# A two-layer image kernel: last stage with its 192 inner channels divided as 128 and 64, images split in seven strips

## The chip, the core and the metric

The kernel runs on one core of a Trainium2 chip. The metric is the time of the whole program on the device in microseconds (us), the median of the runs. PE is the matrix engine (PEld its weight loads), DVE the vector engine, ACT the scalar engine, POOL the GpSimd engine, SP the engine whose queue issues all the transfers here.

## The reference, cut to what matters

The program applies two layers to 32 images of 56 x 56 pixels with 48 channels: an adapter with a convolution whose weights are generated, then a block with window attention and a feed-forward part. The change lies in the feed-forward part alone:

```python
x = shortcut + o                       # (32, 56, 56, 48), after the attention
y = _layer_norm(x, ln2_g, ln2_b)
y = conv(y, w_ffn1)                    # 3 x 3, 48 -> 192 channels, 'SAME'
y = gelu(y * bn1_scale + bn1_shift)    # exact gelu
y = conv(y, w_ffn2)                    # 1 x 1, 192 -> 48 channels
return x + (y * bn2_scale + bn2_shift)
```

## The kernel before, in words

The program has three stages that follow one another with a barrier between them: the adapter, the attention (which leaves `x2_chunks`, the residual, and `y_chunks`, the normalized input of the feed-forward part, in device memory), and `feed_forward`, the last stage. Only the last is changed.

**Data of an image.** The 48 channels times 3 rows of the 3 x 3 window make 144 values for each pixel. 128 of them stand in the tile `ya` as partitions (three copies of the image, each shifted by a row), the last 16 in `yb`, three times (shifted by a column), so 48 partitions with data, of 64. Each row has 58 columns (`YW`), so an image is 3248 columns. There is one `ya` and one `yb`. Nine transfers fill each of them (`Y_DMAS`).

**Precision.** Matmuls work on a short float format (`F32R`). Each factor is divided into an upper part (a cast, `hi`) and the rest (a subtraction, `lo`), and a product is the sum of hi x hi, lo x hi and hi x lo. The split images `ya_hi`, `ya_lo` and `yb_sp` (hi and lo of `yb` in one tile) exist twice, one for even and one for odd images (`a` is 0 or 1).

**Loops.** An image is worked on in 7 strips of 8 rows, 448 pixels each (`C1` is 7, `T1` is 448). For each strip and each half of the 192 inner channels (k = 0, 1; 96 channels each) `convolve` issues 11 matmuls: three columns of the window times three products from `ya`, and two from `yb_sp`. That is 22 for a strip. ACT computes the gelu of the half (line 1303) and casts it (1306), POOL subtracts (1233), and `feed_back` multiplies hidden values by `wf` in 6 matmuls for the strip (line 1265), one strip behind the convolution. DVE then adds the scaled result to the residual `xr` (line 1365).

**Splitting the next image.** DVE does it in four pieces of a whole image, after the results of strips 1, 2, 3 and 4: cast of `ya` (1330), cast of `yb` (1333), subtraction for `ya` (1336), subtraction for `yb` (1339). When both subtractions are done SP starts to load the image after that into `ya` and `yb`:

```python
sp.wait_ge(y_lo_set, image * 2 + 4)
load_ya(m + 1, a)
load_yb(m + 1, a)
sp.wait_ge(result, image * C1 + C1)
sp.dma_start(out[image, :, :], xr[a][:, :]).then_inc(out_done[a], 16)
```

DVE also adds the constant `t2` to the whole of `xr` once per image (1357). Each engine works through its own instructions in the written order; semaphores join them.

Of the kernel before, what the change touches and what calls it, by code (L numbers as in the profile page):

```python
# [20 lines left out]
F32 = mybir.dt.float32  # L21
# [9 lines left out]
HID = 4 * C  # L31
N = WS * WS
# [30 lines left out]
class Pack:  # L63
# [34 lines left out]
    "wa": (128, 3 * HID), "wb": (PP, HID), "wf2": (HID // 2, 2 * C),  # L98
    "s1": (HID // 2, 2), "t1": (HID // 2, 2), "s2": (C, 1), "t2": (C, 1),
# [1006 lines left out]
def feed_forward(nc, x2s, ys, pack, out):  # L1106
# [7 lines left out]
    with ctx:  # L1114
# [39 lines left out]
        def by_column(tile):  # L1154
            return tile[:, :].rearrange("q (k m) -> q k m", k=3)
# [4 lines left out]
        def _(sp):  # L1160
# [43 lines left out]
            sp.wait_ge(y_lo_set, 2)  # L1204
            load_ya(0, 1)
            load_yb(0, 1)
            with sp.Fori(0, B // 2 - 1) as m:
                for a in range(2):
                    image = m * 2 + a
                    sp.wait_ge(y_lo_set, image * 2 + 4)  # L1210
# [12 lines left out]
        @block.gpsimd  # L1223
        def _(pool):

            for row in (0, H - 1):
                ins = pool.memset(ya[:, row * YW:(row + 1) * YW], 0.0)  # L1227
            ins.then_inc(ya_zeroed, 1)

            def images(m):  # L1230
                for U in range(4 * C1):
                    pool.wait_ge(hid_hi_set, m * (4 * C1) + U + 1)  # L1232
                    pool.tensor_tensor(hid_lo[:, U % slots, :], hid[:, U % slots, :], hid_hi[:, U % slots, :],  # L1233
                                       ALU.subtract).then_inc(hid_lo_set, 1)

            with pool.Fori(0, B // 2) as m:  # L1236
                images(m)

        @block.tensor
        def _(pe):  # L1240
            def convolve(bank, a, c, k):
                rows = slice(c * R1, (c + 1) * R1)
                hidden = slice(k * half, (k + 1) * half)

                def pixels(tile, kw):
                    return tile.rearrange("q (r n) -> q r n", r=H)[:, rows, kw:kw + W]

                for kw in range(3):
                    for i, (weights, image) in enumerate(((wa_hi, ya_hi), (wa_hi, ya_lo), (wa_lo, ya_hi))):
                        pe.matmul(ps_h[bank][0:half, 0:T1], by_column(weights)[:, kw, hidden],  # L1250
                                  pixels(image[a][:, :], kw), start=kw == 0 and i == 0, stop=False)

                pe.matmul(ps_h[bank][0:half, 0:T1], wb_hi[:, hidden], pixels(yb_sp[a][:, :], 0), start=False, stop=False)
                pe.matmul(ps_h[bank][0:half, 0:T1], wb_lo[:, hidden], pixels(yb_sp[a][:, :], 0),  # L1254
                          start=False, stop=True).then_inc(h_mm, 1)

            def feed_back(t, T):

                pe.wait_ge(hid_lo_set, 2 * t + 2)
                if not isinstance(t, int) or t >= 2:  # L1260
                    pe.wait_ge(result, t - 1)
                for k in range(2):
                    slot, m = (2 * T + k) % slots, slice(k * C, (k + 1) * C)
                    for i, (weights, hidden) in enumerate(((wf_hi, hid_hi), (wf_lo, hid_hi), (wf_hi, hid_lo))):
                        mm = pe.matmul(ps_f[T % 2][0:C, 0:T1], weights[:, m], hidden[:, slot, :],  # L1265
                                       start=k == 0 and i == 0, stop=k == 1 and i == 2)
                mm.then_inc(f_mm, 1)

            def images(m):

                for a in range(2):
                    start = isinstance(m, int) and a == 0
                    if start:
                        pe.wait_ge(first_lo_set, 2)
                    else:
                        pe.wait_ge(y_lo_set, m * 4 + a * 2 + 2)
                    for c in range(C1):
                        if start and c == first_rows // R1:
                            pe.wait_ge(y_lo_set, 2)
                        T = a * C1 + c  # L1280
                        t = m * (2 * C1) + T
                        for k in range(2):
                            if not isinstance(m, int) or t * 2 + k >= slots:
                                pe.wait_ge(gelu_done, t * 2 + k - slots + 1)
                            convolve((2 * T + k) % slots, a, c, k)
                        if not isinstance(m, int) or t >= 1:
                            feed_back(t - 1, (T - 1) % (2 * C1))

            pe.wait_ge(w_lo_set, 3)
            images(0)  # L1290
            with pe.Fori(1, B // 2) as m:
                images(m)
            feed_back(B * C1 - 1, 2 * C1 - 1)

        @block.scalar
        def _(act):
            def images(m):
                for U in range(4 * C1):
                    u = m * (4 * C1) + U
                    act.wait_ge(h_mm, u + 1)  # L1300
                    if not isinstance(m, int) or u >= slots:
                        act.wait_ge(f_mm, m * (2 * C1) + (U - slots) // 2 + 1)
                    act.activation(hid[:, U % slots, :], ps_h[U % slots][0:half, 0:T1], ACT.Gelu,  # L1303
                                   bias=w("t1")[:, U % 2:U % 2 + 1], scale=w("s1")[:, U % 2:U % 2 + 1]).then_inc(gelu_done, 1)
                    act.wait_ge(gelu_done, u + 1)
                    act.activation(hid_hi[:, U % slots, :], hid[:, U % slots, :], ACT.Copy).then_inc(hid_hi_set, 1)  # L1306

            act.wait_ge(weights_in, 16)
            images(0)
            with act.Fori(1, B // 2) as m:  # L1310
                images(m)

        @block.vector
        def _(dve):
# [3 lines left out]
            dve.memset(yb[BO // 2:BO, 0:(H - 1) * YW - 2], 0.0).then_inc(yb_zeroed, 1)  # L1318
            dve.wait_ge(weights_in, 16)
            dve.tensor_copy(wa_hi[:, :], w("wa")).then_inc(w_hi_set, 1)  # L1320
            dve.tensor_copy(wb_hi[:, :], w("wb")).then_inc(w_hi_set, 1)
            dve.tensor_copy(wf_hi[:, :], w("wf2")).then_inc(w_hi_set, 1)
            dve.wait_ge(w_hi_set, 3)
            dve.tensor_tensor(wf_lo[:, :], w("wf2"), wf_hi[:, :], ALU.subtract).then_inc(w_lo_set, 1)
            dve.tensor_tensor(wa_lo[:, :], w("wa"), wa_hi[:, :], ALU.subtract).then_inc(w_lo_set, 1)
            dve.tensor_tensor(wb_lo[:, :], w("wb"), wb_hi[:, :], ALU.subtract).then_inc(w_lo_set, 1)


            def split_hi_a(a, px, signal):
                return dve.tensor_copy(ya_hi[a][:, px], ya[:, px]).then_inc(signal, 1)  # L1330

            def split_hi_b(a, px, signal):
                return dve.tensor_copy(yb_sp[a][0:BO, px], yb[:, px]).then_inc(signal, 1)

            def split_lo_a(a, px, signal):
                return dve.tensor_tensor(ya_lo[a][:, px], ya[:, px], ya_hi[a][:, px], ALU.subtract).then_inc(signal, 1)

            def split_lo_b(a, px, signal):
                return dve.tensor_tensor(yb_sp[a][BO:PP, px], yb[0:C, px], yb_sp[a][0:C, px], ALU.subtract).then_inc(signal, 1)  # L1339
# [175 lines left out]
```

## Time and profile before

| | |
|---|---|
| median of three runs | 3990.65 us (3989.6 to 3991.79) |
| profiled execution, its time | 3992.1 us |
| its span | 3990.3 us |
| last stage in that span | from 2627.4 us to the end |
| mean granted clock of PE, share of full speed | 0.972 |
| busy, share of the span | PE 93%, DVE 61%, ACT 59%, POOL 56% |

The busy shares are means over three stages. Matmuls overlap in the pipeline: each lasts about 0.37 us in the records, while the next one starts about 0.2 us after it, so what counts is the distance between starts. Times in the rows are from the start of the span.

### The profile page before, as it was taken

Reading aid. Unit: us, or ns where it says so; the run is one execution under the profiler, and the core shown is the slowest. Engines: PE = TensorE matmul, PEld = TensorE weight load, DVE = VectorE, ACT = ScalarE, POOL = GpSimd, SP = SyncE. Lnnn points to the kernel's source line nnn. Section 1 sums busy time; section 2 is a strip of 40 time slices with the busy share of each in tenths; the row PEclk is TensorE's granted clock in tenths of the full one; section 3 lists DMA queues with packets and bytes.
Section 4 is the critical chain, followed back from the end, with each engine's and each line's share of the span. In section 5 each row is a group of like instructions: output and inputs, shape, how many; then the busy total and the mean of one; then the engine's idle time right before and its main releaser. Section 6 shows DMA issues by size and latency. Waiting matters only on the chain. (4 is left out here: it accounts for less than half of the span.)

```text
span 3990.3 us, 95518 instructions
## 1 busy us (share of the span) xinstructions
PE 3711.8 (93%) x33140; PEld 2678.4 (67%) x33140; DVE 2432.0 (61%) x3923; ACT 2334.6 (59%) x4212; POOL 2240.8 (56%) x2186
## 2 busy tenths in 40 slices
PE   6889789999999999999999999959999999999999
PEld 3556566666666666666666666647777777777776
DVE  4544367777777777777777777743444434444343
ACT  3343167777777777777777777734444444444444
POOL 1111156666666666666666666635655656556564
PEclk7898899999999999999999999979999999999999
DMA  4331111111111111111111111145445454454542
GB/s 105 97 97 48 56 32 37 37 37 37 37 37 39 38 38 38 37 37 37 37 37 37 39 38 38 35 72 99 76 86 88 70 98 75 86 88 70 98 75 47
DMA packets 235743, 229.73 MB, mean 58 GB/s; under 512 B 118064, under 2 KB 230704, under 8 KB 232624
## 3 DMA queue, kind: packets, MB, share of 16 engines
q1 hardware_dynamic: 235696, 229.14, 28.2%
q8 instruction: 26, 0.43, 0.0%
q14 instruction: 21, 0.17, 0.0%
HBM read 151.26 MB, written 77.76 MB: 57 GB/s over the span
## 5 line engine op out<-in xcount | busy, mean ns | idle before, releaser
L1233 POOL TENSOR_TENSOR hid_lo<-hid,hid_hi 96x448 fp32r<-96x448 f32 x448 | 771.2, 1727 | 583.5 <-ACT hid_hi L1306 583.5
L613 POOL TENSOR_TENSOR kex<-ks,cw 112x294 f32<-112x294 f32 x1024 | 734.3, 752 | 232.1 <-ACT ks L865 232.1
L1303 ACT ACTIVATE hid<-ps_h,cw 96x448 f32<-96x448 f32 x448 | 324.0, 723 | 728.0 <-PE ps_h L1254 728.0
L1365 DVE SCALAR_TENSOR_TENSOR xr<-ps_f,cw,xr 48x448 f32<-48x448 f32 x224 | 151.3, 676 | 773.2 <-PE ps_f L1265 773.2
L673 PE MATMUL ps_s<-kex,qbd 112*98 112x294 f32 x2048 | 591.9, 410 | 0.0
L1250 PE MATMUL ps_h<-ya_hi,wa_hi 128*96 128x448 f32 x1344 | 501.4, 373 | 30.1 <-DVE yb_sp L1339 30.1
L1250 PE MATMUL ps_h<-ya_hi,wa_lo 128*96 128x448 f32 x1344 | 498.4, 371 | 0.0
L1250 PE MATMUL ps_h<-ya_lo,wa_hi 128*96 128x448 f32 x1344 | 498.2, 371 | 0.0
L1012 DVE TENSOR_TENSOR s<-ps_s,bias 98x294 f32<-98x294 f32 x1024 | 434.9, 454 | 14.1 <-PE ps_s L673 2.1
L673 PEld LDWEIGHTS ps_s<-kex,qbd 112*98 112x98 f32 x2048 | 318.0, 165 | 165.8 <-issue 80.2
L888 ACT ACTIVATE pt<-ps_t 98x588 f32<-98x588 f32 x512 | 338.6, 661 | 120.1 <-PE ps_t L684 114.5
L1024 DVE TENSOR_REDUCE mx<-s 98x12 f32<-98x588 f32 x512 | 390.7, 763 | 13.2
L1028 DVE TENSOR_TENSOR s<-s,mx 98x588 f32<-98x588 f32 x384 | 388.6, 1012 | 13.1
L684 PEld LDWEIGHTS ps_t<-cw,s 98*98 98x98 f32 x3072 | 300.3, 126 | 101.7 <-issue 46.5
L881 ACT ACTIVATE s<-s 98x588 f32<-98x588 f32 x512 | 354.4, 692 | 4.2 <-DVE s L1028 1.1
L684 PE MATMUL ps_t<-cw,s 98*98 98x98 f32 x3072 | 347.8, 248 | 1.3 <-ACT lnv L901 1.3
L699 PEld LDWEIGHTS ps_o<-vs,pt 98*49 98x49 f32 x12288 | 303.2, 126 | 66.1 <-issue 53.4
L699 PE MATMUL ps_o<-vs,pt 98*49 98x18 f32 x12288 | 328.5, 199 | 0.0
L1250 PEld LDWEIGHTS ps_h<-ya_hi,wa_hi 128*96 128x96 f32 x1344 | 216.8, 161 | 102.4 <-issue 30.7
L744 PEld LDWEIGHTS ps_m<-wvs,h 112*98 112x98 f32 x2048 | 197.9, 167 | 108.7 <-issue 100.9
L1306 ACT ACTIVATE hid_hi<-hid 96x448 fp32r<-96x448 f32 x448 | 259.1, 578 | 14.3
L1250 PEld LDWEIGHTS ps_h<-ya_hi,wa_lo 128*96 128x96 f32 x1344 | 217.2, 162 | 65.3
(152 smaller groups left out, 6767.4 us busy)
## 6 DMA issues: line engine op xcount, KB each, us to landing
ya<-y_chunks SPq DMA_DIRECT2D x64, 532.9 KB, 6.4
y_chunks<-y SPq DMA_DIRECT2D x256, 76.1 KB, 1.8
xin<-x_chunks SPq DMA_DIRECT2D x256, 73.5 KB, 2.5
xres<-x_chunks SPq DMA_DIRECT2D x256, 73.5 KB, 1.9
x_chunks<-xo SPq DMA_DIRECT2D x256, 73.5 KB, 1.8
out<-xr SPq DMA_DIRECT2D x32, 588.0 KB, 8.2
yb<-y_chunks SPq DMA_DIRECT2D x96, 177.6 KB, 8.2
xr<-x_chunks SPq DMA_DIRECT2D x32, 514.5 KB, 5.6
```

The source lines that it names most:

```text
L613: pool.tensor_tensor(kex[a][:, win, :, :], ks[:, win, :].unsqueeze(1).to_broadcast([PP, HEADS, N]), w("head").unsqueeze(2).to_broadcast([P ...
L673: pe.matmul(ps_s[win % 3][0:2 * N, 0:HN], qbd[a][:, win, :], kex[a][:, win, :, :].rearrange("c h k -> c (h k)"), start=True, stop=True).th ...
L684: mm = pe.transpose(ps_t[0:2 * N, i, part], s_sb[d % 2][:, i, part], w("ident"))
L699: mm = pe.matmul(ps_o[BO * img:BO * img + N, (i * (HEADS // 2) + j) * VW:(i * (HEADS // 2) + j + 1) * VW], pt[win // 2][:, win % 2, j, img ...
L881: act.activation(s_sb[d % 2][:, :, :], s_sb[d % 2][:, :, :], ACT.Exp).then_inc(exp_done, 1)
L888: act.activation(pt[d][:, :, :, :, :].rearrange("q w j i n -> q w (j i n)"), ps_t[0:2 * N, :, 0:HN], ACT.Copy).then_inc(pt_set, 1)
L1012: dve.tensor_tensor(s_sb[i][:, k, :], ps_s[win % 3][0:2 * N, 0:HN], bias[:, low, int(win == NWC - 1), :], ALU.add).then_inc(s_biased, 1)
L1024: dve.tensor_reduce(mxi, s4, AX.X, ALU.max).then_inc(max_done, 1)
L1028: dve.tensor_tensor(s4, s4, mxi.unsqueeze(2).to_broadcast([2 * N, 2 * HEADS, N]), ALU.subtract).then_inc(shifted, 1)
L1233: pool.tensor_tensor(hid_lo[:, U % slots, :], hid[:, U % slots, :], hid_hi[:, U % slots, :], ALU.subtract).then_inc(hid_lo_set, 1)
L1250: pe.matmul(ps_h[bank][0:half, 0:T1], by_column(weights)[:, kw, hidden], pixels(image[a][:, :], kw), start=kw == 0 and i == 0, stop=False)
L1303: act.activation(hid[:, U % slots, :], ps_h[U % slots][0:half, 0:T1], ACT.Gelu, bias=w("t1")[:, U % 2:U % 2 + 1], scale=w("s1")[:, U % 2:U ...
```

## The change: what it does

- The inner channels are divided as 128 (part a) and 64 (part b) instead of 96 and 96. For part b the upper and lower halves of the weights stand side by side in one tile (`wa_both`, `wb_both`, 2 x 64 columns). One matmul with `ya_hi` then gives hi x hi in 64 rows of the result and lo x hi in the other 64. Part b takes 7 matmuls (`convolve_b`), part a 11 (`convolve_a`).
- ACT copies the other 64 rows of part b out of the matmul's result (`upper_half`), DVE adds the two halves (`add_halves_b`), and the gelu reads the sum.
- `feed_back` has the halves of `wf` side by side too: 3 matmuls, two strips behind the convolution, and its result stands in two halves that DVE adds one after the other (`add_result`, two instructions).
- The image is split in seven strips of 464 columns, one in each slot (a slot is the work for one strip of results), instead of four whole-image pieces. Casts and the subtraction for `yb` stay on DVE, the subtraction for `ya` goes to POOL (`split_lo_a`). POOL keeps the subtraction for part a of the hidden values; that for part b is on DVE.
- The constant `t2` is added by ACT, strip by strip (`add_shift`).
- SP loads the next `ya` when all seven strips are subtracted (`y_a_set`), and `yb` on `y_b_set`. There is still one `ya` and one `yb`.

```diff
+            sp.wait_ge(y_a_set, image * slices + 2 * slices)
             load_ya(m + 1, a)
+            sp.wait_ge(y_b_set, image * slices + 2 * slices)
             load_yb(m + 1, a)
...
         @block.gpsimd
...
+            def split_lo_a(image, a, s):
+                pool.wait_ge(ya_hi_set, image * slices + s + 1)
+                pool.tensor_tensor(ya_lo[a][:, strip(s)], ya[:, strip(s)], ya_hi[a][:, strip(s)], ALU.subtract).then_inc(y_a_set, 1)
...
+            def slots(m, last):
+                for T in range(images):
...
+                    if started(t, 1):
+                        hidden_lo(t - 1, (T - 1) % images)
...
+                    if not (last and a == 1):
+                        split_lo_a(m * 2 + a + 1, 1 - a, c)
...
         @block.tensor
...
+            def convolve_b(t, T, a, c):
+                if started(t, 2):
+                    pe.wait_ge(b_added, t - 1)
+                bank = ps_b[T % 2]
+                pe.matmul(bank[:, 0:T1], wb_both[:, :], pixels(yb_sp[a][:, :], c, 0), start=True, stop=False)
+                for kw in range(3):
+                    pe.matmul(bank[0:HB, 0:T1], wa_both[:, kw, 0:HB], pixels(ya_lo[a][:, :], c, kw), start=False, stop=False)
+                for kw in range(3):
+                    mm = pe.matmul(bank[:, 0:T1], wa_both[:, kw, :], pixels(ya_hi[a][:, :], c, kw), start=False, stop=kw == 2)
+                mm.then_inc(b_mm, 1)
...
+                    elif c == 0:
+                        pe.wait_ge(y_a_set, (m * 2 + a) * slices + slices)
+                        pe.wait_ge(y_b_set, (m * 2 + a) * slices + slices)
+                    convolve_b(t, T, a, c)
+                    convolve_a(t, T, a, c)
+                    if started(t, 2):
+                        feed_back(t - 2, (T - 2) % images)
...
         @block.scalar
...
+            def slots(m):
+                for T in range(images):
+                    t = m * images + T
+                    upper_half(t, T)
+                    if started(t, 1):
+                        hidden_a(t - 1, (T - 1) % images)
+                        add_shift(m if T >= 1 else m - 1, (T - 1) % images)
+                    hidden_b(t, T)
...
         @block.vector
...
+            def split(image, a, s):
+                px = strip(s)
+                if s == 0:
                     dve.wait_ge(ya_in, image * (Y_DMAS * 16) + Y_DMAS * 16)
+                dve.tensor_copy(ya_hi[a][:, px], ya[:, px]).then_inc(ya_hi_set, 1)
+                if s == 0:
                     dve.wait_ge(yb_in, image * (Y_DMAS * 16) + Y_DMAS * 16)
+                dve.tensor_copy(yb_sp[a][0:BO, px], yb[:, px]).then_inc(yb_hi_set, 1)
+                dve.wait_ge(yb_hi_set, image * slices + s + 1)
+                dve.tensor_tensor(yb_sp[a][BO:PP, px], yb[0:C, px], yb_sp[a][0:C, px], ALU.subtract).then_inc(y_b_set, 1)
...
+            def slots(m, last):
+                for T in range(images):
+                    t = m * images + T
+                    if started(t, 3):
+                        add_result(t - 3, (T - 3) % images)
+                    if started(t, 1):
+                        hidden_lo(t - 1, (T - 1) % images)
+                    a, c = T // C1, T % C1
+                    add_halves_b(t, T)
+                    if not (last and a == 1):
+                        split(m * 2 + a + 1, 1 - a, c)
```

On DVE, in the loop over images, this stood around the start of a split before (`ya_in` and `yb_in` count landed transfers, `f_mm` finished `feed_back`s):

```order
L1357 TENSOR_SCALAR xr<-xr,cw 48x3136 [waits x2_in0]
L1361 ISA
L1363 ISA [waits shift_added]
L1365 SCALAR_TENSOR_TENSOR xr<-ps_f,cw,xr 48x448 [waits f_mm]
L1363 REGISTER_ALU
L1365 SCALAR_TENSOR_TENSOR xr<-ps_f,cw,xr 48x448 [waits f_mm]
L1343 ISA
L1330 CAST ya_hi<-ya 128x3248 [waits ya_in]
L1363 REGISTER_ALU
L1365 SCALAR_TENSOR_TENSOR xr<-ps_f,cw,xr 48x448 [waits f_mm]
L1333 CAST yb_sp<-yb 64x3248 [waits yb_in]
```

And this stands there now, from the first strip of an image's slots (where the split of the next image starts) into the second:

```order
L1423 SCALAR_TENSOR_TENSOR xr<-ps_f,cw,xr 48x448 [waits f_mm,shift_added]
L1426 SCALAR_TENSOR_TENSOR xr<-ps_f,cw,xr 48x448 [waits f_half_added]
L1415 TENSOR_TENSOR hid_b_sp<-hid_b,hid_b_sp 64x448 [waits b_hi_set]
L1410 REGISTER_ALU
L1411 TENSOR_TENSOR pre<-ps_b,small 64x448 [waits small_set]
L1401 ISA
L1402 CAST ya_hi<-ya 128x464 [waits ya_in]
L1405 CAST yb_sp<-yb 64x464 [waits yb_in]
L1406 ISA
L1407 TENSOR_TENSOR yb_sp<-yb,yb_sp 48x464 [waits yb_hi_set]
L1423 SCALAR_TENSOR_TENSOR xr<-ps_f,cw,xr 48x448 [waits f_mm,shift_added]
```

The wait for the transfers moved from the second strip of an image to its first, and results and sums of later strips stand behind it.

POOL, in its loop, had one kind of work before:

```order
L1233 TENSOR_TENSOR hid_lo<-hid,hid_hi 96x448 [waits hid_hi_set]
L1232 REGISTER_ALU
L1233 TENSOR_TENSOR hid_lo<-hid,hid_hi 96x448 [waits hid_hi_set]
L1232 REGISTER_ALU
L1233 TENSOR_TENSOR hid_lo<-hid,hid_hi 96x448 [waits hid_hi_set]
```

and has two kinds in turn now:

```order
L1248 TENSOR_TENSOR hid_a_lo<-hid_a,hid_a_hi 128x448 [waits a_hi_set]
L1243 ISA
L1244 TENSOR_TENSOR ya_lo<-ya,ya_hi 128x464 [waits ya_hi_set]
L1247 REGISTER_ALU
L1248 TENSOR_TENSOR hid_a_lo<-hid_a,hid_a_hi 128x448 [waits a_hi_set]
```

The number of its instructions for a strip stays at two; the second one of a slot now follows DVE's cast of the same strip, and releases the loads.

## Rows read from the trace of the kernel before

**Rows 1.** The page: span, and each engine's busy time (share, instructions).
```profile
span 3990.3 us, 95518 instructions
PE 3711.8 (93%) x33140; PEld 2678.4 (67%) x33140; DVE 2432.0 (61%) x3923; ACT 2334.6 (59%) x4212; POOL 2240.8 (56%) x2186
```
**Rows 2.** Busy time by stretch: one image, twenty images; clock, DMA share, GB/s last.
```profile
3024.60:3066.10 41.50, 40.90 (x197) 29.90 (x196) 17.55 (x12) 18.22 (x28) 24.28 (x15) 1.00 0.47 83
3066.10:3901.00 834.90, 822.84 (x3939) 600.78 (x3937) 351.67 (x241) 365.70 (x562) 489.11 (x282) 1.00 0.48 83
```
**Rows 3.** Timeline of PE (start, duration, line): first matmuls of two strips.
```profile
3001.70 0.37 PE L1250 MATMUL ps_h<-ya_hi,wa_hi 128*96 128x448 f32 x1
...
3007.51 0.38 PE L1250 MATMUL ps_h<-ya_hi,wa_hi 128*96 128x448 f32 x1
```
**Rows 4.** Groups by line, 2700 to 3900 us: count | busy, mean ns | idle before.
```profile
L1303 ACT ACTIVATE hid<-ps_h,cw 96x448 f32<-96x448 f32 x404 | 292.2, 723 | 661.0 <-PE ps_h L1254 661.0
L1306 ACT ACTIVATE hid_hi<-hid 96x448 fp32r<-96x448 f32 x404 | 233.6, 578 | 12.9
```
**Rows 5.** Timeline of SP's queue: first ya, last ya, last yb transfer; next image's first.
```profile
3024.61 0.33 SPq L1170 DMA_DIRECT2D ya<-y_chunks  x1
3028.51 0.32 SPq L1179 DMA_DIRECT2D ya<-y_chunks  x1
3032.89 0.32 SPq L1179 DMA_DIRECT2D yb<-y_chunks  x1
3066.15 0.33 SPq L1170 DMA_DIRECT2D ya<-y_chunks  x1
```
**Rows 6.** Tile yb: time from a transfer's issue to its landing.
```profile
DMA to landing us min/median/max: 6.7/8.1/10.8
```
**Rows 7.** Timeline of DVE at the stage's start: split of the first rows.
```profile
2643.01 0.64 DVE L1330 CAST ya_hi<-ya 128x928 fp32r<-128x928 f32 x1 [7.29 <-DMA ya<-y_chunks]
2643.69 1.13 DVE L1336 TENSOR_TENSOR ya_lo<-ya,ya_hi 128x928 fp32r<-128x928 f32 x1
2648.82 0.64 DVE L1333 CAST yb_sp<-yb 64x928 fp32r<-64x928 f32 x1 [4.00 <-DMA yb<-y_chunks]
```
**Rows 8.** Timeline of DVE in the loop.
```profile
3001.90 0.68 DVE L1365 SCALAR_TENSOR_TENSOR xr<-ps_f,cw,xr 48x448 f32<-48x448 f32 x1 [5.15 <-PE ps_f L1265]
3002.50 1.83 DVE L1330 CAST ya_hi<-ya 128x3248 fp32r<-128x3248 f32 x1
3014.14 3.52 DVE L1336 TENSOR_TENSOR ya_lo<-ya,ya_hi 128x3248 fp32r<-128x3248 f32 x1
3020.89 3.54 DVE L1339 TENSOR_TENSOR yb_sp<-yb,yb_sp 48x3248 fp32r<-48x3248 f32 x1
```
**Rows 9.** The page's groups: a DVE sum with one input from PSUM.
```profile
L1012 DVE TENSOR_TENSOR s<-ps_s,bias 98x294 f32<-98x294 f32 x1024 | 434.9, 454 | 14.1 <-PE ps_s L673 2.1
```
**Rows 10.** Timeline of POOL beside rows 8.
```profile
3002.09 3.27 POOL L1233 TENSOR_TENSOR hid_lo<-hid,hid_hi 96x448 fp32r<-96x448 f32 x1 [1.08 <-ACT hid_hi L1306]
3005.67 1.15 POOL L1233 TENSOR_TENSOR hid_lo<-hid,hid_hi 96x448 fp32r<-96x448 f32 x1 [0.32 <-ACT hid_hi L1306]
3013.74 7.16 POOL L1233 TENSOR_TENSOR hid_lo<-hid,hid_hi 96x448 fp32r<-96x448 f32 x3 [1.08 <-ACT hid_hi L1306]
```
**Rows 11.** Timelines of POOL and DVE in the attention stage, then that DVE line's min/median/max ns.
```profile
2549.69 1.02 POOL L621 TENSOR_TENSOR y<-xc,rstd 112x392 f32<-112x392 f32 x1 [1.68 <-ACT rstd L907]
2550.02 1.32 DVE L1028 TENSOR_TENSOR s<-s,mx 98x588 f32<-98x588 f32 x1
L1028 DVE TENSOR_TENSOR s<-s,mx x384: 770/773/1341, 519.4 to 2600.5; 98x588 f32<-98x588 f32 x192
```
**Rows 12.** Stretches at the start of the stage's matmuls; columns as in rows 2.
```profile
2650.80:2654.20 3.40, 3.40 (x10) 2.55 (x10) 3.40 (x3) 0.00 (x0) 0.00 (x0) 0.50 0.42 63
2654.20:2658.00 3.80, 3.80 (x20) 2.94 (x19) 3.77 (x2) 3.08 (x4) 0.41 (x1) 1.00 0.02 4
```
**Rows 13.** Timelines of DVE and SP: last result, last transfer.
```profile
3984.07 0.68 DVE L1365 SCALAR_TENSOR_TENSOR xr<-ps_f,cw,xr 48x448 f32<-48x448 f32 x1 [2.15 <-PE ps_f L1265]
3984.77 0.34 SPq L1219 DMA_DIRECT2D out<-xr  x1
```

More of the change, by code:

```diff
@@ L31 @@
 HID = 4 * C
+HA, HB = 128, HID - 128
 N = WS * WS
@@ L1239, in _, with pixels @@
+            pool.wait_ge(weights_in, 16)
+            for s in range(slices):
+                split_lo_a(0, 0, s)
+            slots(0, False)
+            with pool.Fori(1, B // 2 - 1) as m:
+                slots(m, False)
+            slots(B // 2 - 1, True)
+            hidden_lo(LAST, images - 1)
         @block.tensor
         def _(pe):
[L1241 to L1246, printed above, removed]
+            def pixels(tile, c, kw):
+                return tile.rearrange("q (r n) -> q r n", r=H)[:, c * R1:(c + 1) * R1, kw:kw + W]
@@ L1248, in convolve, with convolve_a @@
+            def convolve_a(t, T, a, c):
+                if started(t, 2):
+                    pe.wait_ge(gelu_a_done, t - 1)
+                bank = ps_a[T % 2]
                 for kw in range(3):
                     for i, (weights, image) in enumerate(((wa_hi, ya_hi), (wa_hi, ya_lo), (wa_lo, ya_hi))):
-                        pe.matmul(ps_h[bank][0:half, 0:T1], by_column(weights)[:, kw, hidden],
-                                  pixels(image[a][:, :], kw), start=kw == 0 and i == 0, stop=False)
@@ L1253, in convolve @@
-                pe.matmul(ps_h[bank][0:half, 0:T1], wb_hi[:, hidden], pixels(yb_sp[a][:, :], 0), start=False, stop=False)
-                pe.matmul(ps_h[bank][0:half, 0:T1], wb_lo[:, hidden], pixels(yb_sp[a][:, :], 0),
-                          start=False, stop=True).then_inc(h_mm, 1)
+                        pe.matmul(bank[:, 0:T1], weights[:, kw, :], pixels(image[a][:, :], c, kw), start=kw == 0 and i == 0, stop=False)
+                pe.matmul(bank[:, 0:T1], wb_hi[:, :], pixels(yb_sp[a][:, :], c, 0), start=False, stop=False)
@@ L1257, in feed_back @@
+                pe.matmul(bank[:, 0:T1], wb_lo[:, :], pixels(yb_sp[a][:, :], c, 0), start=False, stop=True).then_inc(a_mm, 1)
             def feed_back(t, T):
-                pe.wait_ge(hid_lo_set, 2 * t + 2)
-                if not isinstance(t, int) or t >= 2:
+                pe.wait_ge(b_lo_set, t + 1)
+                pe.wait_ge(a_lo_set, t + 1)
+                if started(t, 2):
                     pe.wait_ge(result, t - 1)
[L1262 to L1287, printed above, removed]
@@ L1291, in _, with hidden_a @@
+            pe.wait_ge(w_lo_set, 6)
+            slots(0)
             with pe.Fori(1, B // 2) as m:
-                images(m)
-            feed_back(B * C1 - 1, 2 * C1 - 1)
+                slots(m)
+            feed_back(LAST - 1, images - 2)
+            feed_back(LAST, images - 1)
         @block.scalar
         def _(act):
[L1297 to L1306, printed above, removed]
+            def hidden_a(t, T):
+                act.wait_ge(a_mm, t + 1)
+                if started(t, 2):
+                    act.wait_ge(a_lo_set, t - 1)
+                act.activation(hid_a[:, T % 2, :], ps_a[T % 2][:, 0:T1], ACT.Gelu, bias=w("t1a"), scale=w("s1a")).then_inc(gelu_a_done, 1)
+                act.wait_ge(gelu_a_done, t + 1)
+                if started(t, 2):
+                    act.wait_ge(f_mm, t - 1)
+                act.activation(hid_a_hi[:, T % 2, :], hid_a[:, T % 2, :], ACT.Copy).then_inc(a_hi_set, 1)
@@ L1308, in _ @@
             act.wait_ge(weights_in, 16)
-            images(0)
+            slots(0)
             with act.Fori(1, B // 2) as m:
-                images(m)
+                slots(m)
+            hidden_a(LAST, images - 1)
+            add_shift(B // 2 - 1, images - 1)
         @block.vector
@@ L1324, in _ @@
[L1324 to L1333, printed above, removed]
@@ L1359, in image_done @@
-            def image_done(m, a, split_next):
-                image = m * 2 + a
-                dve.wait_ge(shift_added, image + 1)
-                for c in range(C1):
-                    dve.wait_ge(f_mm, image * C1 + c + 1)
-                    cols = slice(c * T1, (c + 1) * T1)
-                    dve.scalar_tensor_tensor(out=xr[a][:, cols], in0=ps_f[(a * C1 + c) % 2][0:C, 0:T1], scalar=w("s2"),
-                                             in1=xr[a][:, cols], op0=ALU.mult, op1=ALU.add).then_inc(result, 1)
-                    if split_next and 1 <= c <= 4:
-                        split(image + 1, 1 - a, c - 1)
@@ L1391, in program @@
+            for s in range(slices):
+                split(0, 0, s)
+            slots(0, False)
+            with dve.Fori(1, B // 2 - 1) as m:
+                slots(m, False)
+            slots(B // 2 - 1, True)
+            add_result(LAST - 2, images - 3)
+            hidden_lo(LAST, images - 1)
+            add_result(LAST - 1, images - 2)
+            add_result(LAST, images - 1)
 def program(nc, x, pack1, pack2, pack3, out):
```

164 lines of the change are left out of this document (93 added, 71 removed).

## The prediction, written before the changed kernel ran

> **What bounds the kernel now.** I read the page first: PE is busy 93% of the span [rows 1]. Then the last stage by stretches: in one image of it, and in twenty, PE is busy for 98.5% at a full clock, while DVE, ACT and POOL stand at 42 to 59% [rows 2]. PE is the bound there. The timeline gives its price: 5.81 us between the first matmuls of two strips, with 28 matmuls between (22 and 6), so 0.2075 us for each [rows 3]. An image takes 41.54 us, from one first `ya` transfer to the next [rows 5], though 7 x 5.81 is 40.7: PE waits about 0.9 us for POOL. Last I read the transfers, since the change moves their wait.
>
> **What PE gains.** A strip has 7 + 11 + 3 = 21 matmuls now: 21 x 0.2075 = 4.36 us, 30.5 us an image. Weight loads of 128 columns are not in the trace of this stage; those of 96 hide behind the matmuls, and I leave the distance at 0.2075. If this were still the bound, each image would save 11 us. I don't think it will be.
>
> **DVE's strip.** The casts: 0.64 us for 928 columns, 1.83 for 3248 [rows 7, 8], so 0.40 for 464. The subtraction: 1.13 and 3.52, so 0.65 for 464 and 0.63 for 448 [rows 7, 8]. The sum with one input from PSUM: 0.454 for 294 columns [rows 9], at the same slope 0.61 for 448. A result costs 0.68 [rows 8], now twice. Together 0.68 + 0.68 + 0.63 + 0.61 + 0.40 + 0.40 + 0.65 = 4.05. An instruction with nothing to wait for starts 0.08 before the end of the last (3001.90 + 0.68 against 3002.50); that applies to 5 of the 7. One that waits for its predecessor starts 0.04 later [rows 7]; that applies to 2. So 4.05 - 0.40 + 0.08 = 3.73 us a strip, under PE's 4.36.
>
> **ACT's strip.** Gelu 0.72 twice, casts 0.58 twice [rows 4], two more instructions of about 0.58: 3.8 us with the waits inside it. It has cover, and it hides the copy and the shift. `add_shift` moves off DVE for nothing.
>
> **The wait that takes over.** There is one `ya` and one `yb`. Before, DVE split an image after results 1 to 4, and about three strips passed between the last subtraction (3020.89 + 3.54 = 3024.43) and the next cast that needs the loaded data, which hid the load. Now the seventh strip is split in the seventh slot and the first strip of the next image in the very next slot, so the whole load stands open. Its length: 0.2 us until SP issues (3024.43 to 3024.61), 8.28 us from the first `ya` transfer to the last `yb` transfer [rows 5], 8.1 us until that lands [rows 6]: 16.6 us. Behind the waiting cast on DVE stand the cast and subtraction of `yb`, then results, `hidden_lo` and sums of the next strips. PE can go on for about two and a half strips, until `feed_back` wants the `hidden_lo` that stands behind the wait. PE cannot start the next image either, since it wants all seven strips of it split.
>
> So an image is now one loop: load, then what is left of the first strip (cast 0.40 and subtraction 0.65 of `yb`, 1.0 with the overlaps), then six slots of DVE, whose last cast frees POOL's last subtraction, which releases the load. With six slots at 3.73 and the last subtraction of POOL ending 0.3 after the slot, that is 16.6 + 1.0 + 22.4 + 0.3 = 40.3 us, hardly under the 41.54 of before. PE's work fits in it with 10 us to spare.
>
> **POOL and DVE get in each other's way.** A subtraction on POOL takes 1.15 us alone. One that met a cast of 1.83 us on DVE took 3.27, and three that met a subtraction of 3.52 us took 7.16, where 3 x 1.15 is 3.45 [rows 8, 10]: POOL stands still while DVE casts or subtracts. It goes the other way too: line 1028 takes 0.77 us at its best, and 1.32 in the place where a POOL instruction had begun 0.33 us before; it was held until about 2550.57, just before that one ended at 2550.71 [rows 11]. So these two cannot run together, while a result or the sum (one input from PSUM) can run beside POOL. A slot has 0.63 + 0.40 + 0.40 + 0.65 = 2.08 us of exclusive DVE work and two POOL subtractions of about 1.07 us hold each (the 3.27 ended 1.03 after the cast). Who goes first decides the slot:
> - If the subtraction for `ya`, ready when the first cast ends, gets its turn in the gap between the cast of `yb` and the subtraction of `yb` (DVE waits there for its own cast), DVE loses 1.05 us in each slot. POOL's other subtraction meets `hidden_lo` or the cast every second slot: another 0.1 or 0.4. Slots of about 4.85 and 5.25, 5.0 in the mean and 4.8 for the first, whose hidden work is already done: 29.8 for six.
> - If it waits for the end of the slot, it runs beside the two results, and only the other one costs DVE 0.5: five slots of 4.25 and one of 3.73, 25.0.
>
> I take the first, because the instruction that waits longest is POOL's, and line 1028 was held for nearly the whole of what was left of a POOL instruction. The Trainium skill, page "SBUF — State Buffer", section "Who interferes with whom", says that whoever issues first keeps the shared ports for the whole instruction and the other blocks fully. Rows 11 agree. Rows 10 agree less: POOL's instruction is recorded 0.41 us before DVE's cast and yet stood still. By the rule the time is the 4162 us below, by a right of way for DVE the 4061.
>
> **The sum.** Loop of an image: 16.6 + 1.0 + 29.8, less 0.4 since POOL's last subtraction ends before DVE's: 47.0 us. Start: the first cast of `yb` could begin at 2648.82 [rows 7]; 1.0 for the first strip, then six strips back to back at 0.32 + 0.32 + 1.07 + 0.57 = 2.3, all exclusive: released at about 2663. Thirty-one loops: 1457. The last image has no split, so PE sets it: 30.5, and 2 for a halved clock after the wait (the first 3.4 us of the stage's matmuls ran at 0.50, then it rose to 1.00 [rows 12]; PE's gap of some 6 us will let it fall again, elsewhere hidden by the spare). Then the tail of the last strip: 10 us (gelu, cast and POOL's subtraction 2.5, `feed_back` 0.8, two results 1.4, transfer out 5.5, from 3984.77 to the span's end at 3990.3 [rows 1, 13]). Span: 2663 + 1457 + 42.5 = 4162.5. The profiled execution lasted 1.8 us more than its span, and its 3992.1 stands 1.45 above the median; so 4163 as a median.
>
> **Rivals.**
> - B, DVE keeps its turn: 16.6 + 1.0 + 25.0 + 1.1 = 43.7 an image; 2663 + 31 x 43.7 + 42.5 + 0.4 = 4061. For it: rows 10. Against it: rows 11.
> - C, the other side: POOL's work falls into DVE's waits and costs nothing, so the loop is the 40.3 above, start at 2658. 2658 + 1249 + 42.5 = 3950, faster. It decides below 41.5 an image, that is if contention costs less than 0.2 us a slot, or if the load lands some 3 us sooner. Against it: 2.08 + 2.14 us of exclusive work in a slot of 3.73.
> - D, PE stays the bound because the load hides after all: 30.5 to 31 an image, 3670. The order of the waits speaks against it.
> - E, the clock stays at half for most of an image: 7 x 8.7 = 61 an image, about 4600. For it: PE idle for a third of the loop. Against it: the rise after 3.4 us of work in rows 12.
> - F, dearer meetings (each DVE instruction held, 5.7 a slot): 51 an image, 4290.
>
> **Chances and range.** My forecast 45%, B 25%, C 14%, D 3%, E 4%, F 9%. Unknown costs: slot 3.73 to 5.7, load 15 to 17.5 us (31 us for each us). The range goes from the middle of C to short of F, 3955 to 4260; for slower cases alone 4020 to 4230. A change below 0.2% (8 us) could not be told from none. Faster: most of C, and D, 15%; within: 3%; slower: 82%.
>
> **What would show it.** In the new profile DVE waits some 12 us for the `yb` transfers once an image, the first `ya` transfers stand about 47 us apart (43.7 for B, 40.3 for C), PE's busy share in the stage falls to two thirds, and the subtraction of `yb` for a strip starts about 1.1 us after the cast before it. No wait for the transfers would prove the central step wrong. A distance of matmuls above 0.3 us would make PE a bound again.

## The result, and the profile after

The changed kernel takes 4264.3 us (median of 4 runs, 4261.3 to 4266.9) against 3990.6 us (4 runs, 3989.6 to 3991.8): 1.0685 times as long, 95% interval 1.0667 to 1.0704. The forecast was slower, 4163 us, with 3955 to 4260 as the range: the direction and the cause held, the size was 101 us short, and the time lies 4 us above the range.

The page of the changed kernel, its span and engines, answers to [rows 1]:

```profile
span 4264.7 us, 93986 instructions
PE 3550.4 (83%) x31572; PEld 2623.3 (62%) x31572; DVE 3028.0 (71%) x5111; ACT 2583.7 (61%) x4660; POOL 2008.3 (47%) x2186
```

PE lost 161 us of work and the span grew by 274, so no engine's busy time tells why. The stretches do (columns as in [rows 2]; twenty-nine images of the last stage, then three stretches of 4 us around the start of one):

```profile
2707.10:4168.80 1461.70, 1045.43 (x4263) 816.84 (x4263) 1053.45 (x1422) 756.60 (x1218) 488.41 (x406) 0.86 0.42 69
3076.00:3080.00 4.00, 0.06 (x1) 0.06 (x1) 3.09 (x6) 0.00 (x0) 0.00 (x0) 0.74 0.00 0
3080.00:3084.00 4.00, 4.00 (x11) 3.09 (x12) 3.90 (x6) 3.31 (x6) 1.34 (x2) 0.50 0.00 0
3084.00:3088.00 4.00, 4.00 (x19) 3.33 (x18) 3.90 (x6) 2.12 (x4) 2.37 (x2) 0.91 0.72 141
```

PE is busy for 71.5% of the stage where it was 98.5%. After 4.7 us without work (from 3075.2 to 3079.9) its granted clock is at 0.50, the lower level, for 4 us, and 0.91 in the next four. DVE, too, is busy for only 72%: no engine is the bound, a loop through several is. SP's queue (start, duration; the loop's first transfer, then first `ya` and last `yb` of one image, the first of the next, and the last image's) answers to [rows 5]:

```profile
2660.44 0.32 SPq L1180 DMA_DIRECT2D ya<-y_chunks  x1
...
3060.35 0.33 SPq L1180 DMA_DIRECT2D ya<-y_chunks  x1
...
3068.70 0.32 SPq L1189 DMA_DIRECT2D yb<-y_chunks  x1
...
3110.80 0.33 SPq L1180 DMA_DIRECT2D ya<-y_chunks  x1
...
4168.75 0.33 SPq L1180 DMA_DIRECT2D ya<-y_chunks  x1
```

From the first to the last of these, 30 images, the first transfers stand 50.3 us apart in the mean (forecast 47.0, before 41.5). DVE's timeline over the same image, from the load's end into the slots:

```profile
3072.50 0.40 DVE L1402 CAST ya_hi<-ya 128x464 fp32r<-128x464 f32 x1 [7.38 <-DMA ya<-y_chunks]
3076.75 0.39 DVE L1405 CAST yb_sp<-yb 64x464 fp32r<-64x464 f32 x1 [3.84 <-DMA yb<-y_chunks]
...
3077.84 0.68 DVE L1423 SCALAR_TENSOR_TENSOR xr<-ps_f,cw,xr 48x448 f32<-48x448 f32 x1
...
3082.74 0.68 DVE L1423 SCALAR_TENSOR_TENSOR xr<-ps_f,cw,xr 48x448 f32<-48x448 f32 x1
...
3084.17 1.40 DVE L1415 TENSOR_TENSOR hid_b_sp<-hid_b,hid_b_sp 64x448 fp32r<-64x448 f32 x1
3085.60 0.62 DVE L1411 TENSOR_TENSOR pre<-ps_b,small 64x448 f32<-64x448 f32 x1
3086.14 0.38 DVE L1402 CAST ya_hi<-ya 128x464 fp32r<-128x464 f32 x1
3086.45 0.39 DVE L1405 CAST yb_sp<-yb 64x464 fp32r<-64x464 f32 x1
3086.87 1.52 DVE L1407 TENSOR_TENSOR yb_sp<-yb,yb_sp 48x464 fp32r<-48x464 f32 x1
3088.42 0.68 DVE L1423 SCALAR_TENSOR_TENSOR xr<-ps_f,cw,xr 48x448 f32<-48x448 f32 x1
```

The load takes 16.4 us from the first transfer to the cast of `yb`, and DVE stands idle for 11.2 of them. Then come the rest of the first strip (1.1 us), a first slot of 4.90, and five of 5.68 (3082.74 to 3088.42), where 5.0 was expected. The subtraction of `yb` takes 1.52 us instead of 0.64, and `hidden_lo` (line 1415) takes 1.40 where it takes 0.62 alone. What POOL did in that slot:

```profile
3083.94 1.14 POOL L1248 TENSOR_TENSOR hid_a_lo<-hid_a,hid_a_hi 128x448 fp32r<-128x448 f32 x1 [1.73 <-ACT hid_a_hi L1338]
3086.60 1.29 POOL L1244 TENSOR_TENSOR ya_lo<-ya,ya_hi 128x464 fp32r<-128x464 f32 x1 [1.52 <-DVE ya_hi L1402]
```

POOL's instruction is recorded first in both meetings (by 0.23 and 0.27 us) and ends 0.5 us before DVE's, which needs 0.62 or 0.64 alone. The views by line (min/median/max in ns) say that this is the rule and no accident of one slot:

```profile
L1407 DVE TENSOR_TENSOR yb_sp<-yb,yb_sp x224: 634/1510/1530, 2646.7 to 4217.7; 48x464 fp32r<-48x464 f32 x112
...
L1415 DVE TENSOR_TENSOR hid_b_sp<-hid_b,hid_b_sp x224: 609/1405/1442, 2677.5 to 4254.4; 64x448 fp32r<-64x448 f32 x112
```

The waits from 2800 to 4000 us (in total, times, longest), 24 images long:

```profile
PE ps_b L1277 <- DVE yb_sp L1407: 186.5, 24, 7.8
DVE ya_hi L1402 <- DMA ya<-y_chunks: 175.4, 24, 7.7
DVE yb_sp L1405 <- DMA yb<-y_chunks: 91.6, 24, 4.4
PE ps_f L1301 <- DVE hid_b_sp L1415: 97.7, 24, 5.0
```

Once an image DVE waits for the load, PE for the last of seven strips, and PE again for the `hidden_lo` that stands behind DVE's wait.

### The profile page after: what moved, and what is told of

It is laid out like the page before. It is cut to its first block and busy times, and to the rows that moved or that the text cites. A ratio compares the mean times of both kernels' runs of the same rounds, so it can differ in the third digit from the quotient of the medians.

```text
span 4264.7 us, 93986 instructions
## 1 busy us (share of the span) xinstructions
PE 3550.4 (83%) x31572; PEld 2623.3 (62%) x31572; DVE 3028.0 (71%) x5111; ACT 2583.7 (61%) x4660; POOL 2008.3 (47%) x2186
## 5 line engine op out<-in xcount | busy, mean ns | idle before, releaser
L1244 POOL TENSOR_TENSOR ya_lo<-ya,ya_hi 128x464 fp32r<-128x464 f32 x224 | 283.3, 1265 | 622.2 <-DVE ya_hi L1402 622.2
L1346 ACT ACTIVATE hid_b<-pre,cw 64x448 f32<-64x448 f32 x224 | 170.2, 760 | 573.9 <-DVE pre L1411 573.9
L1248 POOL TENSOR_TENSOR hid_a_lo<-hid_a,hid_a_hi 128x448 fp32r<-128x448 f32 x224 | 257.1, 1148 | 469.5 <-ACT hid_a_hi L1338 469.5
L1290 PE MATMUL ps_a<-ya_hi,wa_hi 128*128 128x448 f32 x672 | 278.4, 414 | 73.2 <-ACT hid_a L1334 73.0
L1277 PE MATMUL ps_b<-yb_sp,wb_both 112*128 112x448 f32 x224 | 104.5, 466 | 274.9 <-DVE yb_sp L1407 270.1
L1407 DVE TENSOR_TENSOR yb_sp<-yb,yb_sp 48x464 fp32r<-48x464 f32 x224 | 310.2, 1385 | 7.8
L1290 PE MATMUL ps_a<-ya_lo,wa_hi 128*128 128x448 f32 x672 | 265.0, 394 | 0.0
L1415 DVE TENSOR_TENSOR hid_b_sp<-hid_b,hid_b_sp 64x448 fp32r<-64x448 f32 x224 | 259.9, 1160 | 7.0
L1290 PE MATMUL ps_a<-ya_hi,wa_lo 128*128 128x448 f32 x672 | 261.0, 388 | 0.0
```

Source lines behind the costliest of these rows:

```text
L1244: pool.tensor_tensor(ya_lo[a][:, strip(s)], ya[:, strip(s)], ya_hi[a][:, strip(s)], ALU.subtract).then_inc(y_a_set, 1)
L1248: pool.tensor_tensor(hid_a_lo[:, T % 2, :], hid_a[:, T % 2, :], hid_a_hi[:, T % 2, :], ALU.subtract).then_inc(a_lo_set, 1)
L1290: pe.matmul(bank[:, 0:T1], weights[:, kw, :], pixels(image[a][:, :], c, kw), start=kw == 0 and i == 0, stop=False)
```

## The experiments

All are changes of one or two things in the changed kernel ("the base" below, 4264 us, 50.3 us an image). Two doubts led them: is the open load the cause of the loss, and what are the 5.68 us of a slot made of?

**Two tiles each for ya and yb.** Loads run a whole image ahead.

```diff
-        ya = sb("ya", [128, H * YW])
-        yb = sb("yb", [BO, H * YW])
+        ya = [sb(f"ya{a}", [128, H * YW]) for a in range(2)]
+        yb = [sb(f"yb{a}", [BO, H * YW]) for a in range(2)]
...
             sp.wait_ge(y_a_set, slices)
-            load_ya(0, 1)
+            load_ya(1, 0)
```

> The changed kernel with two tiles each for ya and yb, so that an image is loaded a whole image ahead; order and number of DVE's and POOL's instructions unchanged. Theory (the loop of an image is load + first strip + six slots, and the 16.5 us load stands open): the load goes, seven slots of 5.69 us are left, 39.8 us an image, 2660 + 31 x 39.8 + 46 = 3940 us, faster than before the change. Rival (PE at half clock and its own waits set the time, the load only fills time that is lost anyway): 47 us an image or more, above 4150.

Measured: 3921 us (3918 to 3925, 4 runs), 0.983 of before (0.982 to 0.985). One more buffer gives back 343 us: the open load is what made the change a loss. What is left, by the waits from 2800 to 3800 us and by DVE's timeline (lines have moved: 1418 is the subtraction of `yb`, 1426 `hidden_lo`, 1416 the cast of `yb`):

```profile
PE ps_b L1286 <- DVE yb_sp L1418: 164.7, 26, 6.4
```

```profile
3064.84 0.62 DVE L1426 TENSOR_TENSOR hid_b_sp<-hid_b,hid_b_sp 64x448 fp32r<-64x448 f32 x1
...
3066.34 1.35 DVE L1416 CAST yb_sp<-yb 64x464 fp32r<-64x464 f32 x1
3067.72 1.52 DVE L1418 TENSOR_TENSOR yb_sp<-yb,yb_sp 48x464 fp32r<-48x464 f32 x1
```

Now DVE sets the pace, busy for 89% of the stage: most slots take 5.1 to 5.9 us, one of an image 4.4, and one 6.4 or 7.3, in which DVE waits for what PE starts late. That makes 39.2 us an image; the time is 19 us under what I expected. A meeting that misses `hidden_lo` holds the cast instead.

**The casts in another order.** `yb` is cast and subtracted first, `ya` cast last, so POOL's subtraction for `ya` becomes ready when DVE turns to results, which read PSUM.

```diff
-                dve.tensor_copy(ya_hi[a][:, px], ya[:, px]).then_inc(ya_hi_set, 1)
...
                 dve.tensor_tensor(yb_sp[a][BO:PP, px], yb[0:C, px], yb_sp[a][0:C, px], ALU.subtract).then_inc(y_b_set, 1)
+                if s == 0:
+                    dve.wait_ge(ya_in, image * (Y_DMAS * 16) + Y_DMAS * 16)
+                dve.tensor_copy(ya_hi[a][:, px], ya[:, px]).then_inc(ya_hi_set, 1)
```

> The changed kernel with DVE's order in a strip turned: cast of yb, subtraction of yb, then cast of ya, so that POOL's subtraction for ya becomes ready after DVE's last exclusive instruction. Theory (POOL takes its turn in DVE's gap and holds the subtraction of yb for 0.87 us a slot): that hold goes, slots of 4.6 to 4.8, 46 us an image, about 4130. Rival (the subtraction lasts 1.5 us for another reason, its shape or partitions): 4264 as before and 1.5 us still.

Measured: 4128.6 us, 1.035 of before (1.033 to 1.037). From the third on, a slot is 4.33 us (DVE):

```profile
3059.94 0.62 DVE L1415 TENSOR_TENSOR hid_b_sp<-hid_b,hid_b_sp 64x448 fp32r<-64x448 f32 x1
3060.59 0.62 DVE L1411 TENSOR_TENSOR pre<-ps_b,small 64x448 f32<-64x448 f32 x1
3061.13 0.70 DVE L1402 CAST yb_sp<-yb 64x464 fp32r<-64x464 f32 x1
3061.86 0.64 DVE L1404 TENSOR_TENSOR yb_sp<-yb,yb_sp 48x464 fp32r<-48x464 f32 x1
3062.53 0.40 DVE L1407 CAST ya_hi<-ya 128x464 fp32r<-128x464 f32 x1
3062.85 0.67 DVE L1423 SCALAR_TENSOR_TENSOR xr<-ps_f,cw,xr 48x448 f32<-48x448 f32 x1
```

and POOL in it:

```profile
3060.30 1.28 POOL L1248 TENSOR_TENSOR hid_a_lo<-hid_a,hid_a_hi 128x448 fp32r<-128x448 f32 x1 [0.41 <-ACT hid_a_hi L1338]
3063.01 1.21 POOL L1244 TENSOR_TENSOR ya_lo<-ya,ya_hi 128x464 fp32r<-128x464 f32 x1 [1.44 <-DVE ya_hi L1407]
```

The subtraction of `yb` is back at 0.64 us. POOL's work for `ya` runs beside the results, whose 0.67 and 0.69 us are unchanged. Its hidden subtraction runs beside the sum (0.62, unchanged) and holds only the cast, by 0.31; `hidden_lo`, which is recorded 0.36 us before it, keeps its 0.62. So two-SBUF-input instructions and casts are held, and those with an input from PSUM are not. Six slots take 26.7 us in place of 33.3 (the first two are 4.86 and 4.52 long, since POOL is late from the first strip and holds `hidden_lo` and then the cast for longer). That saves 6.6 us, and an image only 4.4: POOL's last subtraction now ends 1.3 us after the slot instead of 0.5 before it (1.8 back), and the cast of `ya` stands behind the load too (0.3). So the 4130 that I had expected is in part luck: the slots are shorter than the 4.6 to 4.8 of that sum, 4.45 in the mean, and what comes back at the end of an image was not in it.

**POOL's subtraction for the hidden values cut short**, first alone, then with the one for `ya`. These kernels leave out lo parts of the products, so they serve to measure and not to use.

```diff
-                pool.tensor_tensor(hid_a_lo[:, T % 2, :], hid_a[:, T % 2, :], hid_a_hi[:, T % 2, :], ALU.subtract).then_inc(a_lo_set, 1)
+                pool.tensor_tensor(hid_a_lo[:, T % 2, 0:8], hid_a[:, T % 2, 0:8], hid_a_hi[:, T % 2, 0:8], ALU.subtract).then_inc(a_lo_set, 1)
...
```

> The changed kernel with only POOL's subtraction of the hidden values cut to 8 columns (that lo part is left out). Theory (each of POOL's two instructions holds one of DVE's): the subtraction of the hidden values on DVE returns from 1.41 to 0.62 us, that of yb stays at 1.5, slots of 4.9 us, 46.3 us an image, about 4140. Rival (POOL's backlog is the cause, so that one shorter instruction frees both): slots near 4.0 us, below 4050.

Measured: 4139.9 us, 1.038 of before (1.036 to 1.040). DVE:

```profile
3059.82 0.68 DVE L1424 SCALAR_TENSOR_TENSOR xr<-ps_f,cw,xr 48x448 f32<-48x448 f32 x1
...
3061.25 0.62 DVE L1416 TENSOR_TENSOR hid_b_sp<-hid_b,hid_b_sp 64x448 fp32r<-64x448 f32 x1
...
3063.17 1.53 DVE L1408 TENSOR_TENSOR yb_sp<-yb,yb_sp 48x464 fp32r<-48x464 f32 x1
3064.73 0.68 DVE L1424 SCALAR_TENSOR_TENSOR xr<-ps_f,cw,xr 48x448 f32<-48x448 f32 x1
```

`hidden_lo` takes 0.62 us, the slot 4.91. That meeting cost 0.78 in five slots of 31 images, 121 us, and 124 are gone. The other one stays at 1.53. Both cut short:

> The changed kernel with both of POOL's subtractions cut to 8 columns (the lo parts of ya and of the 128 hidden channels are left out, their tiles are zero). Theory (POOL holds DVE for 0.87 + 0.80 us a slot, and the load stands open whatever the slots cost): slots of 4.0 us, 16.5 + 1.1 + 24.2 = 42 us an image, 4000 to 4010, still not faster than before the change. Rival (holds do not matter because PE or ACT paces the slot): 47 us or more, above 4150.

Measured: 3968.0 us, 0.995 of before (0.993 to 0.997). I had expected at least 4000, not faster than before. The slots are as expected, but POOL's short last subtraction ends 0.65 us before the next result (at 3059.30, the result at 3059.95), so the load is released sooner: an image takes 41.0 us for 42. DVE's timeline, and its longest wait from 2800 to 3800 us:

```profile
3039.86 0.68 DVE L1429 SCALAR_TENSOR_TENSOR xr<-ps_f,cw,xr 48x448 f32<-48x448 f32 x1
...
3043.21 0.64 DVE L1413 TENSOR_TENSOR yb_sp<-yb,yb_sp 48x464 fp32r<-48x464 f32 x1
3043.88 0.68 DVE L1429 SCALAR_TENSOR_TENSOR xr<-ps_f,cw,xr 48x448 f32<-48x448 f32 x1
```

```profile
DVE ya_hi L1408 <- DMA ya<-y_chunks: 204.0, 24, 8.9
```

The slot without any meeting is 4.02 us, not the 3.73 that I had built from durations. Meetings cost 296 us together, 172 of them the one with the subtraction of `yb` (6 x 31 x 0.88 = 164); the load is as open as before. Without meetings and with the open load the kernel is half a per cent faster than before; without the open load but with meetings, 1.7.

**The split later.** One buffer, no strip split in the first three slots, then 1, 2, 2, 2, so that the load has slots to hide behind.

```diff
+        strips_in_slot = [[], [], [], [0], [1, 2], [3, 4], [5, 6]]
...
-                        split(m * 2 + a + 1, 1 - a, c)
+                        for s in strips_in_slot[c]:
+                            split(m * 2 + a + 1, 1 - a, s)
```

> The changed kernel with one buffer, but the seven strips split in the last four slots of an image (1, 2, 2 and 2) and none in the first three. Theory: the load then runs beside three slots and more of other work, some 14 of its 16.5 us are covered, 39 to 41 us an image, 3930 to 3990. If instead the work on DVE and POOL sets the time wherever the split stands (a sum of 5.69 x 7 = 39.8 plus crowding), the same 39.8 is its floor too; if the load is not the cause, 50 us an image and 4260.

Measured: 4024.0 us, 1.009 of before (1.007 to 1.011), 42.5 us an image: 34 us over the upper end of what I expected. DVE waits for no transfer any more, so that step is right. The slots with two strips are dearer than I had put them (DVE; 1404 is the cast of `ya`, 1409 the subtraction of `yb`), and PE waits for their end (waits from 2800 to 3800 us):

```profile
3020.13 1.47 DVE L1409 TENSOR_TENSOR yb_sp<-yb,yb_sp 48x464 fp32r<-48x464 f32 x1
3021.64 1.29 DVE L1404 CAST ya_hi<-ya 128x464 fp32r<-128x464 f32 x1
...
3023.27 1.52 DVE L1409 TENSOR_TENSOR yb_sp<-yb,yb_sp 48x464 fp32r<-48x464 f32 x1
```

```profile
PE ps_b L1279 <- DVE yb_sp L1409: 222.1, 23, 9.7
```

Three meetings in a slot of 8.25 us (first results at 3016.57 and 3024.82): POOL's hidden subtraction, begun at 3019.95, holds the first, and its two for `ya`, begun at 3021.07 and 3023.01, the others. An earlier slot shows a meeting the other way round, which I come back to below.

**Two buffers and the new order together**, the edits of the first two experiments.

> Both edits together: two tiles each for ya and yb, and in a strip the cast and subtraction of yb ahead of the cast of ya. Theory (load and holds are the two costs and add up): DVE's slot of 4.3 us is below PE's 4.4, so PE is the bound again, with a wait of about 1 us at the start of each image for the last strip's subtraction on POOL: 32 us an image, 2655 + 31 x 32 + 45 = 3690. Rival (the two edits save the same time): about 3790 to 3920.

Measured: 3779.5 us (3777 to 3788, 4 runs), 0.948 of before (0.946 to 0.950). The direction is right, the size 90 us off. The savings of the two edits add up, as the theory had it: 343 and 136 make 479, and 485 are measured. What is off is the wait at the start of an image. PE's timeline at the start of an image shows what I had left out:

```profile
3007.30 0.74 PE L1286 MATMUL ps_b<-yb_sp,wb_both 112*128 112x448 f32 x1 [2.99 <-POOL ya_lo L1253]
```

PE waits for the seventh strip, the last thing that POOL does in an image, though it needs the first. That pause costs more than itself: in the 2.8 us behind it (3007.30 to 3010.10) PE's granted clock is 0.50 and it starts 8 matmuls, for which it needs 1.7 us at the upper level. I had put the pause at 1 us and the clock at nothing.

**PE waits for one strip at a time**, on top of that.

```diff
...
-                    elif c == 0:
-                        pe.wait_ge(y_a_set, (m * 2 + a) * slices + slices)
-                        pe.wait_ge(y_b_set, (m * 2 + a) * slices + slices)
+                    pe.wait_ge(y_a_set, (m * 2 + a) * slices + c + 1)
+                    pe.wait_ge(y_b_set, (m * 2 + a) * slices + c + 1)
```

> As both edits together, and PE waits for the one strip that it is about to read instead of all seven at the start of an image. Theory: the wait at the start of an image goes, 21 matmuls at 0.208 us set the time: 30.8 us an image, 2655 + 31 x 30.8 + 45 = 3655. Rival (PE is paced by ACT or DVE in every slot, not at the start of an image): no difference from both edits together.

Measured: 3659.8 us (3654 to 3663, 4 runs), 0.917 of before (0.916 to 0.919). A stretch of 700 us in its last stage (columns as in [rows 2]):

```profile
2800.00:3500.00 700.00, 700.00 (x3342) 589.65 (x3341) 673.92 (x1115) 596.08 (x955) 372.60 (x319) 1.00 0.65 111
```
PE is busy throughout at the upper clock, an image takes 30.8 us (forecast for a bound PE: 30.5), a slot 4.38 (casts of `yb` at 3011.40 and 3015.78), and DVE has 4% left. This is the version to keep: it beats both kernels.

**The same waits without one of the other two edits.** First one buffer with the new order and the waits strip by strip:

> One ya and one yb, casts of yb first, and PE waits for one strip instead of seven at the start of an image. My theory: while the load is open, the loop of an image is load and DVE's slots, and PE is not on it; so when PE may start changes nothing: 45.7 us an image and 4128 us, as with the order alone, within 5 us. Rival: PE's late start also delays what DVE does behind the load (DVE waited 2.9 us an image for the sum with one buffer), then 43 us an image and about 4045.

Measured: 4121.6 us, 1.033 of before (1.030 to 1.036): 7 us less than with the order alone, where I had allowed 5; the rival's 4045 is far off. While the load is open, it hardly matters when PE may start. Then two buffers, the waits strip by strip, and the casts in the base's order:

> Two tiles each for ya and yb, PE waits for one strip instead of seven, the casts of ya first as in the changed kernel. My theory: DVE's slot with both meetings, 5.7 us, is the bound once nothing else is: 7 x 5.7 = 39.9 us an image less the slots that miss a meeting, so about 39 us and 3920, hardly another time than two buffers alone. Rival: the wait for seven strips was what the 39.2 us hung on, then 7 x 4.9 = 34.3 and about 3770.

Measured: 3934.3 us, 0.986 of before (0.983 to 0.989), 14 more than I said. Its stretch:

```profile
2800.00:3500.00 700.00, 579.60 (x2581) 426.90 (x2580) 679.67 (x862) 460.66 (x738) 298.83 (x247) 1.00 0.53 86
```

DVE's slot is the base's, 5.68 us (first results at 3065.47 and 3071.15). Seven of them make 39.8; the first transfers stand 39.9 us apart. DVE is the bound, at 97%. So the order of three instructions is worth 274 us here (3934 to 3660) and 136 where the load is open.

## Why the forecast had the direction and not the size

- **PE no longer the bound, its distance unchanged.** Right: matmuls stand 0.21 us apart at a full clock. The halved clock after each pause costs nothing in the loop, as said, since PE idles 28% of it (DVE's one wait behind PE, 1.75 us for `small` at 3062.8, ends before the load has landed); E falls with the 0.91 in the second four microseconds.
- **The load stands open.** Right, and within 0.2 us: 16.4 measured and 16.6 in the sum, which held a reaction of 0.2. Two buffers took it away and with it 343 us. Of the rivals, D falls by this.
- **POOL wins the gap before the subtraction of yb.** Right, and it cost a little less: 0.88 us in place of 1.05. B, in which DVE keeps its turn, falls. The sign that I had named is not there as written: the subtraction is recorded 0.03 us after the end of the cast, and the hold stands in its length, 1.52 us. The rule of the Trainium skill that the forecast leaned on (page "SBUF — State Buffer", section "Who interferes with whom": the first to issue keeps the shared ports, the other blocks) agrees with these slots, where POOL is recorded first each time. It agrees the other way round too. In the run with the late split DVE's subtraction is recorded 0.04 us ahead; it keeps its 0.64 us, and POOL's lasts 1.61 in place of 1.15:

```profile
3015.53 0.64 DVE L1409 TENSOR_TENSOR yb_sp<-yb,yb_sp 48x464 fp32r<-48x464 f32 x1
3015.57 1.61 POOL L1249 TENSOR_TENSOR hid_a_lo<-hid_a,hid_a_hi 128x448 fp32r<-128x448 f32 x1 [3.27 <-ACT hid_a_hi L1340]
```

  In these meetings the order of two starts decides, be it by hundredths of a microsecond, and not a right of way of either engine; those of [rows 10] stay the exception.
- **Six slots at 29.8 us: the step that failed.** They take 33.3 (4.90 and five of 5.68), and 31 times the 3.3 us by which the loop is longer are the 101 us; the start (2660.4 for 2663) and the tail (45.6 for 42.5) cancel. Per slot of 5.68 in place of 5.0:
  - The meeting with `hidden_lo`: 0.78 in each of them, where I had 0.1 or 0.4, 0.22 in my mean (5.0 - 3.73 - 1.05): +0.56. (The 4.85 and 5.25 of the forecast have 5.05 as their mean, not 5.0, which is 8 us of the time.) I had let it drift from slot to slot and fall mostly on the cast. It doesn't drift. ACT begins the gelu when DVE's sum is done (3080.54 in the slot above) and frees POOL 3.3 us later; DVE reaches `hidden_lo` 3.6 us after the same sum. Both chains start from one event, so POOL is 0.2 to 0.3 us ahead each time:

```profile
3080.57 0.76 ACT L1346 ACTIVATE hid_b<-pre,cw 64x448 f32<-64x448 f32 x1 [9.54 <-DVE pre L1411]
...
3083.29 0.58 ACT L1338 ACTIVATE hid_a_hi<-hid_a 128x448 fp32r<-128x448 f32 x1
```

  - The bare slot: 4.02 and not 3.73, +0.29. I gave five of seven instructions an overlap of 0.08 us. Only two have it (3085.60 + 0.62 against 3086.14, and the cast behind it); the others start 0.02 to 0.03 after the end. Those three write at another partition than the instruction before: in the base a result behind the subtraction that writes at partition 64 starts 0.03 late (3086.87 + 1.52, then 3088.42; the same with no meeting, 3043.21 + 0.64, then 3043.88), while in the other order, behind the cast that writes at partition 0, the same result starts 0.08 early (3062.53 + 0.40, then 3062.85). The Trainium skill, page "VectorE: DVE Perf Modes", section "Two Vector instructions with no wait between them", gives a model in which a held instruction starts only when every earlier one has finished, and in which one is held, among other conditions, when its output starts in another quadrant (32 partitions) than the last output. The rows fit it; no run moved an output to test it. For the sum the input from PSUM starts at another partition than the last one too (0 after 64), which is another of the page's conditions, so only the result and `hidden_lo` speak for the output alone.
  - The meeting with the subtraction of `yb`: 0.88 for 1.05, -0.17.
- **Rival C, without meetings faster than before at 3950.** Its slot was too kind. The 0.29 us that the bare slot lacked are 54 us in six slots of 31 images, more than the 41 that C gained, so C comes to an estimated 4004. With both meetings gone the time was 3968, half a per cent faster, because the short instructions also save elsewhere: POOL's last subtraction ends 0.65 us before the next result and not 0.3 after it, 29 us in all, and the first release of the load comes at 2651.5 for 2658.
- **Rival F, 5.7 us a slot, 4290.** This is what happened, for its price: 5.68. I had given it 9% and let the range end short of it. Its mechanism as I wrote it, each DVE instruction held, is not what happened: two are held and three lose an overlap.

What stays open: why in [rows 10] DVE's whole-image cast, and its whole-image subtraction of 3.52 us, kept POOL waiting although POOL's instruction is recorded 0.41 and 0.40 us before them. None of the runs repeats those meetings.

## What to carry over

When work is cut into pieces that all stages share, look at the single buffer at its head: if the last piece of one round and the first of the next stand in neighbouring slots, its load has nothing left to hide behind, and the saving of any engine comes after that. When two engines that hold each other hang on one event, their meeting repeats in every round at full price, and the order of a few instructions decides what it costs (here: let the other engine's input become ready when this one turns to PSUM; 274 us where DVE was the bound, 136 where the load was open). Price a slot from neighbouring starts, not from durations, and let a range reach over every case that the unknown terms allow.

## What the runs showed that I had not expected

- A DVE subtraction took 0.62 alone and 1.40 in a meeting, or 0.64 and 1.52; a cast 0.39 alone and 1.35, or 0.70 where less of POOL's instruction was left. POOL paid little where it was recorded first, 1.14 to 1.29 in place of 1.15 [rows 10], and up to 1.61 where DVE was.
- A wait of 3.0 us on PE at the start of an image, taken away, gave 120 us, 3.9 an image.
